# The tail of a two-layer kernel reordered: own part of the maxima ahead of the statistics, the sums behind the broadcast rows

## Chip, cores and metric

One core of one Trainium2 chip. The metric is the device time of one execution in microseconds (us). The engines are called TensorE (PE in the rows; PEld is its weight load), VectorE (DVE), ScalarE (ACT), GpSimd (POOL) and SyncE (SP, which issues most transfers).

## What is computed

x has 4 batches of 1024 rows and 512 columns, in fp32. Layer 0 is a two-layer network with a residual; 128 of its 512 output columns come from an expert that the batch's index chooses. Layer 1 scores every row, masks the scores by the batch's type, and pools the rows with the softmax of each row's masked scores.

```
h = gelu(x @ fc1_w.T + fc1_b)                       # 512 -> 2048, exact gelu
x = x + concat(h @ fc2_w.T + fc2_b, h @ experts_w[idx].T + experts_b[idx])
score = tanh(x @ W1 + b1) @ v                       # one number per row l
mask[j, l] = l <= j (type 0), l >= j (type 1), l != j (type 2)
p[j, :] = softmax over l of (score[l] where mask, else -1e30)
x[j] = x[j] + sum_l p[j, l] * x[l] / count(mask[j, :])
```

## The kernel before, in words

The batches run one after the other: a first one with its preparations ("first"), a loop over the other three, and a "tail" that has layer 1 of the last batch only. In the loop TensorE works on layer 0 of one batch, and layer 1 of the batch before is cut into small tasks between its products. In the tail no layer 0 is left to run beside these tasks. Every fp32 operand of a large product is split into a high part (a copy by ScalarE that rounds, helper `hi`, L988) and a low part (a subtraction by VectorE, helper `lo`, L1270), and a product is three matmuls (`three`, L770 to L774).

Layer 1 treats the 1024 rows as 8 chunks of 128 rows. The tasks, in the order of their data:

- `xn` (4 in the tail): chunks are transposed on TensorE (L865), and split into xnh and xnl; `full` keeps an unrounded copy for the last sum. xnl is the last reader of the bank.
- `attn`, `score`: tanh and the scores, s8. Behind `score` follows `maxima` (L1428): two scans of running maxima, F8 and G8, with the product DG between them.
- `stats`: three tiny products (L877 to L879), copied to st by VectorE (L1330). Then `row_maxima` (L1436): Ef and t88 from st, mc from t88, then m0 in three steps from s8, G8, F8 and the mask (L1441 to L1444), m8 from m0 and mc (L1446), and t88 less mc (L1447). The semaphore `chain` counts these 11 steps.
- `mT`: m8 gathered (L883, copied at L1335). `bc` 0 and 1: broadcast rows by eight transposes of mT (L889), from which VectorE makes the exponents of P (L1340, four per half) and of W (L1344).
- `expE`: ScalarE's exponential of Ef, then E's copies into the diagonals of E4 by VectorE: three casts (L1352) and a difference (the fourth copy).
- `sums`: 16 matmuls (L894, L895) of E4 with all chunks, copied to Bs.
- `expPW` h: exponentials of a half of P and W on ScalarE, their high parts, and the low parts Pl and Ws on VectorE.
- GpSimd's `row_sums` (L707) makes the terms of the denominators: FS and decay (L712, L713) when the scans are done, two operations behind m8 (L716, L717), and three at the end (L720 to L724) that need the scans of `scan` (L1373, L1375) and three exponentials of `expM`.
- `total` (L899), `den` (L1389), `rd` (L902, L1392, L1394): the reciprocals of the denominators.
- `pool` c: an own part of chunk c (`own_chunk`, three matmuls of P with x) and one matmul of Ws with Bs (L911) in one bank; then VectorE scales it and adds the row itself (L1406), and SyncE writes 256 KB out (L454).

The order in the tail is written out by hand. `TAIL_ORDER` (L98) is TensorE's order and deals the eight banks out; `TAIL_ACT` and `TAIL_DVE` are those of ScalarE and VectorE. Each engine works strictly in its order. `FILLS` matmuls without use (L955) stand ahead of `mT`. `FULL_BEFORE` says how many `full` copies TensorE awaits ahead of a task. The own parts of chunks 0 to 3 run ahead of `rd`, and those of 4 to 7 ahead of their own `pool`:

```
for c in range(BC) if task[0] == "rd" else [task[1]] if task[0] == "pool" and task[1] >= BC else []:
    own_chunk(kind, b, c, at(kind, "p", ("pool", c)))
```

The loop uses the same functions for its tasks, in the places of `POST_P` (L77): in step 3 the broadcast rows, `expE`, the exponentials, `scan` and the first `expPW`; behind them VectorE has the first `add` (L1465), which frees a bank for TensorE's product P2.

## Time and profile before

| | us |
|---|---|
| median of three runs | 778.43 (778.34 to 780.52) |
| the profiled execution | 778.85 |
| its span, first to last instruction | 777.1 |
| TensorE busy in the span | 762.0 (98%) |
| VectorE, ScalarE, GpSimd busy | 404.9, 386.7, 134.2 |
| mean granted clock of TensorE | 0.995 |

A stretch's row gives its length, then each engine's busy time with the number of its instructions, the granted clock of TensorE (1.00 is 2.4 GHz, 0.50 is 1.2 GHz), the share of the DMA engines and GB/s. A timeline's row gives start, duration, engine, line, operation and tiles; "x4" joins four alike, and what stands in brackets is the idle time before it and what ended it. Start times, not durations, give the pace, since neighbours overlap by about 0.1 us. In the chain a piece lasts until the next one takes over.

### The profile page before, as it was taken

To read this page: it belongs to the slowest core of one execution; us is meant where nothing else is said; L and a number is where in the kernel's file an instruction comes from. 1 tells how busy PE (TensorE), PEld (TensorE's weight loads), DVE (VectorE), ACT (ScalarE), POOL (GpSimd) and SP (SyncE) were. 2 spreads that over 40 slices of the span, in tenths; PEclk is the share of its full clock that TensorE was granted. 3 is DMA by queue.
4 is the path that set the end of the run, shared out by engine and by line. 5 is a ranking of instruction groups with operands and counts; after the bars stand their busy time and mean duration, and the time that the engine had idled before them with its cause. 6 is when DMAs were issued, how large, how long until landed. Compare 5 with 4: busy or idle time off the path is not lost.

```text
span 777.1 us, 11514 instructions
## 1 busy us (share of the span) xinstructions
PE 762.0 (98%) x3466; PEld 622.6 (80%) x3466; DVE 404.9 (52%) x713; ACT 386.7 (50%) x665; POOL 134.2 (17%) x199
## 2 busy tenths in 40 slices
PE   8999999999999999999999999999999999999977
PEld 5788888888888888888888888888888888888855
DVE  6965667573445333754536423377245532265676
ACT  6855665453546433543546633446354653344552
POOL 3273230400011121310001022040001111114011
PEclk9999999999999999999999999999999999999998
DMA  6899898877764568867776466885787466687712
GB/s 217 289 338 322 309 340 275 267 231 238 236 202 150 176 203 280 260 205 244 223 238 195 155 206 206 291 248 175 245 249 232 148 198 205 220 279 217 231 54 108
DMA packets 130714, 176.92 MB, mean 228 GB/s; under 512 B 10064, under 2 KB 97632, under 8 KB 130656
## 3 DMA queue, kind: packets, MB, share of 16 engines
q1 hardware_dynamic: 130496, 176.20, 71.2%
q8 instruction: 28, 0.46, 0.2%
q14 instruction: 30, 0.25, 0.1%
q0 software_dynamic: 160, 0.01, 0.0%
HBM read 136.33 MB, written 39.85 MB: 227 GB/s over the span
## 4 chain that ended last, share of the span: by engine, by line
PE 92%; DVE 3%; DMA 2%; ACT 1%; issue 1%; SPq 1%; DVEq 0%
PE y L772 15%; PE y L774 14%; PE y L773 14%; PE hA L772 7%; PE hA L774 7%; PE hA L773 7%; PE hF L772 6%; PE hF L774 5%; PE hF L773 5%; PE j L865 2%; DMA xrb<-in_x 1%; PE j L844 1%; PE j L842 1%; PE j L841 1%; DMA w2c<-exs 1%
## 5 line engine op out<-in xcount | busy, mean ns | idle before, releaser
L772 PE MATMUL y<-hs,w2c 128*128 128x512 f32 x512 | 201.9, 394 | 0.7 <-DMA w2c<-exs 0.5
L774 PE MATMUL y<-hs,w2c 128*128 128x512 f32 x512 | 199.6, 390 | 0.0
L773 PE MATMUL y<-hs,w2c 128*128 128x512 f32 x512 | 199.2, 389 | 0.0
L772 PEld LDWEIGHTS y<-hs,w2c 128*128 128x128 f32 x512 | 96.1, 188 | 22.8 <-DVE hs L1270 2.5
L774 PEld LDWEIGHTS y<-hs,w2c 128*128 128x128 f32 x512 | 96.1, 188 | 20.5
L773 PEld LDWEIGHTS y<-hs,w2c 128*128 128x128 f32 x512 | 96.2, 188 | 19.3
L772 PE MATMUL hA<-xch,w1c 128*128 128x512 f32 x252 | 99.5, 395 | 2.7 <-DVE w1c L1270 1.7
L774 PE MATMUL hA<-xch,w1c 128*128 128x512 f32 x252 | 98.2, 390 | 0.0
L773 PE MATMUL hA<-xcl,w1c 128*128 128x512 f32 x252 | 98.1, 389 | 0.0
L1042 ACT ACTIVATE hst<-hst,bcol 128x512 f32<-128x512 f32 x62 | 43.9, 721 | 85.4 <-DVE hst L1465 85.4
L1270 DVE TENSOR_TENSOR hs<-gb,hs 128x512 fp32r<-128x512 f32 x64 | 43.5, 716 | 64.6 <-ACT hs L988 64.6
L772 PE MATMUL hF<-xch,w1c 128*128 128x512 f32 x190 | 75.6, 398 | 0.3 <-issue 0.3
L774 PE MATMUL hF<-xch,w1c 128*128 128x512 f32 x190 | 74.1, 390 | 0.0
L773 PE MATMUL hF<-xcl,w1c 128*128 128x512 f32 x190 | 74.0, 389 | 0.0
L988 ACT ACTIVATE hs<-hst 128x512 fp32r<-128x512 f32 x64 | 40.4, 632 | 47.2 <-PE y L774 46.8
L1270 DVE TENSOR_TENSOR hs<-hst,hs 128x512 fp32r<-128x512 f32 x64 | 45.2, 706 | 35.9 <-ACT hs L988 34.9
L772 PEld LDWEIGHTS hA<-xch,w1c 128*128 128x128 f32 x252 | 47.3, 188 | 16.0 <-DVE w1c L1270 3.6
L774 PEld LDWEIGHTS hA<-xch,w1c 128*128 128x128 f32 x252 | 47.3, 188 | 10.0
L773 PEld LDWEIGHTS hA<-xcl,w1c 128*128 128x128 f32 x252 | 47.3, 188 | 9.3
L762 POOL TENSOR_TENSOR x1T<-x1T,xnl 128x512 f32<-128x512 f32 x24 | 30.8, 1290 | 136.7 <-DVE x1T L1409 136.7
L1465 DVE TENSOR_TENSOR hst<-hF,hst 128x512 f32<-128x512 f32 x31 | 21.4, 691 | 55.8 <-PE hF L774 55.3
L1042 ACT ACTIVATE gb<-gb,bcol 128x512 f32<-128x512 f32 x31 | 22.4, 724 | 54.3 <-DVE gb L1465 54.2
(286 smaller groups left out, 1093.9 us busy)
## 6 DMA issues: line engine op xcount, KB each, us to landing
w2c<-w2s SPq DMA_DIRECT2D x114, 384.0 KB, 3.5
w1c<-w1s SPq DMA_DIRECT2D x24, 768.0 KB, 4.4
w2c<-exs SPq DMA_DIRECT2D x114, 128.0 KB, 4.0
w1c<-w1s SPq DMA_DIRECT2D x48, 256.0 KB, 3.4
w1c<-w1s SPq DMA_DIRECT2D x24, 512.0 KB, 3.9
x1T<-in_x SPq DMA_DIRECT2D x32, 256.0 KB, 5.8
w1s<-w1c SPq DMA_DIRECT2D x8, 768.0 KB, 4.1
w2s<-w2c SPq DMA_DIRECT2D x16, 384.0 KB, 4.4
```

The source lines that it names most:

```text
L762: nc.gpsimd.tensor_tensor(oo[:, c % OUTS, :], oo[:, c % OUTS, :], xnl[:, c, :].bitcast(f32), ALU.add).then_inc(row_sum, 1)
L772: nc.tensor.matmul(ps, ah, bh, start=first, stop=False, skip_group_check=onto)
L773: nc.tensor.matmul(ps, ah, bl, start=False, stop=False, skip_group_check=onto)
L774: return nc.tensor.matmul(ps, al, bh, start=False, stop=last, skip_group_check=onto)
L841: nc.tensor.matmul(bank[:, :], W1h[:, dc, :], xh[:, dc, :], start=dc == 0, stop=False)
L842: nc.tensor.matmul(bank[:, :], W1l[:, dc, :], xh[:, dc, :], start=False, stop=False)
L844: last = nc.tensor.matmul(bank[:, :], W1h[:, dc, :], xl[:, dc, :], start=False, stop=dc == DC - 1)
L865: last = nc.tensor.transpose(bank[:, i * P:(i + 1) * P], x1T[:, i, c * P:(c + 1) * P], ident[:, :])
L988: return nc.scalar.activation(out_, in_, ACT.Copy)
L1042: nc.scalar.activation(tile, hA[:, :] if order == 4 else tile, ACT.Gelu, bias=bcol[:, R_FC1 + m:R_FC1 + m + 1]).then_inc(gelu_done, 1)
L1270: return nc.vector.tensor_tensor(out_, in_, hi_.bitcast(f32), ALU.subtract)
L1465: nc.vector.tensor_tensor(tile, bank[:, :], tile, ALU.add).then_inc(add_done, 1)
```

## The change

- `maxima` takes m0's three steps over from `row_maxima`, ahead of the statistics, with the wait for the mask. `row_maxima` makes m8 first, then Ef, then t88 less mc; m8 is step 9 of `chain` and Ef step 10.
- GpSimd starts `row_sums` at m8 rather than at the scans: its first two operations move behind it.
- E's three casts become one ScalarE copy of 128x24, behind Ef's exponential, waiting for it. VectorE keeps the fourth copy. E4 is one column per chunk wider so that the copy's pattern is regular.
- The exponentials of `expB` are three tasks now (`expS` the one of t88, first; `expF`, `expD`), and those of P and W, their high parts (`hiP`, `hiW`) and low parts (`loP`, `loW`) are tasks of their own. P's exponential waits for a new semaphore, `P_in`, that VectorE sets behind P's four operations, W's for the bank as before. `total` waits for the exponential of t88 only.
- TensorE: `sums` stands directly behind `bc` 1, and waits for the bank of each later chunk at that chunk's matmuls, not for the last one at its start. Own parts 0 to 3 run ahead of `total`; own part 4 and the four products of chunks 0 to 3 ahead of `den` and `rd`, own part 5 at `rd`, 6 and 7 at their chunks. All four `full` copies are awaited at `total`. The fills are 5, not 6.
- VectorE: `xn` 2 goes behind `mT`, `xn` 3 between the two `bc`, `scan` behind the first low parts. ScalarE: `expM` goes behind the copy of the sums.

The diff, cut to its core:

```diff
@@ -68,7 +68,7 @@
 UNITS = 2 * HC
-WARM, FILLS = 8, 6
+WARM, FILLS = 8, 5
 W2R = 4
 HSR = 3
...
@@ -97,16 +97,20 @@
 X_LOADS = {5: ((0, 1), 3, 2), 7: ((3,), 4, 3), 8: ((2,), 6, 3)}
 TAIL_ORDER = [("ysum", oc) for oc in range(OC)] + [("x1", oc) for oc in range(OC)] + [
     ("xn", 0), ("xn", 1), ("attn",), ("xn", 2), ("xn", 3), ("score",), ("stats",), ("expE",), ("mT",), ("bc", 0), ("bc", 1),
-    ("scan",), ("total",), ("expPW", 0), ("expPW", 1), ("sums",), ("den",), ("rd", 0, CH)] + [("pool", c) for c in range(CH)]
+    ("expPW", 0), ("sums",), ("scan",), ("expPW", 1), ("total",)] + [("pool", c) for c in range(BC)] + [
+    ("den",), ("rd", 0, CH)] + [("pool", c) for c in range(BC, CH)]
+OWN_BEFORE = {("total",): range(BC), ("pool", 0): [4], ("rd", 0, CH): [5], ("pool", 6): [6], ("pool", 7): [7]}
 TAIL_ACT = [("x1", oc) for oc in range(OC)] + [
-    ("xn", 0), ("xn", 1), ("attn",), ("xn", 2), ("xn", 3), ("full", 0), ("full", 1), ("expE",), ("expB",), ("full", 2), ("expM",),
-    ("full", 3), ("exp", 0), ("PW", 0), ("exp", 1), ("sums",), ("PW", 1)]
+    ("xn", 0), ("xn", 1), ("attn",), ("xn", 2), ("xn", 3), ("full", 0), ("full", 1), ("expE",), ("expS",), ("expF",), ("expD",),
+    ("full", 2), ("expP", 0), ("expW", 0), ("hiP", 0), ("hiW", 0), ("full", 3), ("expP", 1), ("hiP", 1), ("sums",), ("expM",),
+    ("expW", 1), ("hiW", 1)]
 TAIL_DVE = [("ysum", 0), ("ysum", 1), ("x1", 0), ("ysum", 2), ("x1", 1), ("ysum", 3), ("x1", 2), ("x1", 3), ("xn", 0),
-            ("xn", 1), ("score",), ("xn", 2), ("stats",), ("mT",), ("expE",), ("xn", 3), ("bc", 0), ("scan",), ("bc", 1),
-            ("expPW", 0), ("total",), ("sums",), ("expPW", 1), ("den",), ("rd", 0, CH)] + [("pool", c) for c in range(CH)]
-FULL_BEFORE = {("bc", 0): 1, ("bc", 1): 2, ("sums",): 3, ("rd", 0, CH): 4}
+            ("xn", 1), ("score",), ("stats",), ("mT",), ("xn", 2), ("expE",), ("bc", 0), ("xn", 3), ("bc", 1), ("loP", 0), ("loW", 0),
+            ("scan",), ("loP", 1), ("sums",), ("total",), ("loW", 1), ("den",), ("rd", 0, CH)] + [("pool", c) for c in range(CH)]
+FULL_BEFORE = {("bc", 0): 1, ("bc", 1): 2, ("total",): 4}
 def body(kind):
...
@@ -708,11 +715,10 @@
                 twice = lambda t: t[:, :].unsqueeze(1).to_broadcast([P, 2, P])
-                gate(pool, chain, b * NCHAIN + (BOTH - NCHAIN))
+                gate(pool, chain, b * NCHAIN + (MAX - NCHAIN))
                 nc.gpsimd.tensor_tensor(upto(FS), twice(s8), upto(FG), ALU.subtract).then_inc(den_in, 1)
                 nc.gpsimd.tensor_tensor(decay[:, :, :], short_of(FG), upto(FG), ALU.subtract).then_inc(den_in, 1)
                 gate(pool, den_in, b * NIN + (2 - NIN))
-                gate(pool, chain, b * NCHAIN + (MAX - NCHAIN))
                 nc.gpsimd.tensor_tensor(short_of(FG), short_of(FG), twice(m8), ALU.add).then_inc(den_in, 1)
                 nc.gpsimd.tensor_tensor(m0[:, :], s8[:, :], m8[:, :], ALU.add).then_inc(den_in, 1)
                 gate(pool, den_exp, b * NEXP + (6 - NEXP))
...
@@ -889,8 +895,9 @@
                         last = nc.tensor.transpose(bank[:, i * P:(i + 1) * P], mT[:, c:c + 1].to_broadcast([P, P]), ident[:, :])
                 elif task[0] == "sums":
                     pe.wait_ge(Elo, b)
-                    wait_used(pe, kind, b, at(kind, place, ("xn", CT - 1)))
                     for c in range(CH):
+                        if c >= CT:
+                            wait_used(pe, kind, b, at(kind, place, ("xn", c - CT)))
                         nc.tensor.matmul(bank[:, :], E4[:, c, :], xnh[:, c, :], start=(c == 0), stop=False)
                         last = nc.tensor.matmul(bank[:, :], E4[:, c, :], xnl[:, c, :], start=False, stop=(c == CH - 1))
                 elif task[0] == "total":
...
@@ -955,8 +962,7 @@
                                 nc.tensor.matmul(idle[:, :], W1h[:, 0, :], x1he[:, 0, :], start=True, stop=True)
                         if task in FULL_BEFORE:
                             pe.wait_ge(xfull_done, FULL_BEFORE[task])
-                        for c in range(BC) if task[0] == "rd" else [task[1]] if task[0] == "pool" and task[1] >= BC else []:
+                        for c in OWN_BEFORE.get(task, []):
                             own_chunk(kind, b, c, at(kind, "p", ("pool", c)))
                         job(kind, b, "p", task, pos)
                     return
...
@@ -1115,28 +1121,48 @@
                 elif task[0] == "expE":
                     act.wait_ge(chain, b * NCHAIN + (EF - NCHAIN))
                     nc.scalar.activation(Ef[:, :], Ef[:, :], ACT.Exp).then_inc(exp_done, 1)
+                    act.wait_ge(exp_done, b * 5 - 4)
+                    hi(groups[:, :, 0:32 * (GROUPS - 1):32], Ef[:, :].unsqueeze(2).to_broadcast([P, CH, GROUPS - 1])).then_inc(Ehi, 1)
                 elif task[0] == "expB":
-                    exps_B(b)
+                    exp_seen(b)
+                    exp_terms(b)
+                    exp_decay(b)
+                elif task[0] == "expS":
+                    exp_seen(b)
+                elif task[0] == "expF":
+                    exp_terms(b)
+                elif task[0] == "expD":
+                    exp_decay(b)
                 elif task[0] == "expM":
                     exps_M(b)
                 elif task[0] == "expPW":
-                    exp_PW(kind, b, place, task[1])
-                    split_PW(kind, b, task[1])
-                elif task[0] == "exp":
-                    exp_PW(kind, b, place, task[1])
-                elif task[0] == "PW":
-                    split_PW(kind, b, task[1])
+                    exp_P(b, task[1])
+                    exp_W(kind, b, place, task[1])
+                    split_PW(kind, b, task[1], 0)
+                    split_PW(kind, b, task[1], 1)
+                elif task[0] == "expP":
+                    exp_P(b, task[1])
+                elif task[0] == "expW":
+                    exp_W(kind, b, place, task[1])
+                elif task[0] in ("hiP", "hiW"):
+                    split_PW(kind, b, task[1], task[0] == "hiW")
                 elif task[0] == "sums":
                     hi(Bs[:, :], bank[:, :]).then_inc(sumhi, 1)
...
@@ -1328,7 +1358,6 @@
                         maxima(b)
                 elif task[0] == "stats":
                     nc.vector.tensor_copy(st[:, :], bank[:, 0:2 * CH + 1]).then_inc(used, 1)
-                    dve.wait_ge(mask_done, b)
                     wait_used(dve, kind, b, pos)
                     row_maxima(b)
                 elif task[0] == "mT":
...
@@ -1337,8 +1366,9 @@
                     for i in range(CT):
                         c = task[1] * CT + i
-                        nc.vector.scalar_tensor_tensor(Pf[:, c * P:(c + 1) * P], bank[:, i * P:(i + 1) * P], st[:, c:c + 1],
-                                                       TM[:, TRI], ALU.add, ALU.add)
+                        last = nc.vector.scalar_tensor_tensor(Pf[:, c * P:(c + 1) * P], bank[:, i * P:(i + 1) * P], st[:, c:c + 1],
+                                                              TM[:, TRI], ALU.add, ALU.add)
+                    last.then_inc(P_in, 1)
                     half = slice(task[1] * TT, (task[1] + 1) * TT)
                     cross = TM[:, P + task[1] * CT:P + (task[1] + 1) * CT]
                     nc.vector.scalar_tensor_tensor(
...
@@ -1346,30 +1376,21 @@
                         st[:, 2 * CH:2 * CH + 1], cross.unsqueeze(2).to_broadcast([P, CT, P]), ALU.add, ALU.add
                     ).then_inc(used, 1)
                 elif task[0] == "expE":
-                    diagonal = E4[:, :, :].rearrange("p c n -> p (c n)")
-                    dve.wait_ge(exp_done, b * 5 - 4)
-                    for gr in range(GROUPS - 1):
-                        last = nc.vector.tensor_copy(diagonal[:, 32 * gr:32 * gr + (CH - 1) * (P + 1) + 1:P + 1], Ef[:, :])
-                    last.then_inc(Ehi, 1)
                     dve.wait_ge(Ehi, b)
-                    gr = GROUPS - 1
-                    lo(diagonal[:, 32 * gr:32 * gr + (CH - 1) * (P + 1) + 1:P + 1], Ef[:, :],
-                       diagonal[:, 0:(CH - 1) * (P + 1) + 1:P + 1]).then_inc(Elo, 1)
+                    lo(groups[:, :, 32 * (GROUPS - 1)], Ef[:, :], groups[:, :, 0]).then_inc(Elo, 1)
                 elif task[0] == "expPW":
-                    h = task[1]
-                    half, cs = slice(h * TT, (h + 1) * TT), slice(h * BC, (h + 1) * BC)
-                    dve.wait_ge(PWhi, b * 4 + (2 * h - 3))
-                    lo(Pl[:, cs, :].rearrange("p c n -> p (c n)"), Pf[:, half], Ph[:, cs, :].rearrange("p c n -> p (c n)")
-                       ).then_inc(Plo, 1)
-                    dve.wait_ge(PWhi, b * 4 + (2 * h - 2))
-                    third = Ws[64:96, cs, :].rearrange("p c n -> p (c n)")
-                    lo(third, Wf[64:96, half], third).then_inc(Wlo, 1)
+                    split_P(b, task[1])
+                    split_W(b, task[1])
+                elif task[0] == "loP":
+                    split_P(b, task[1])
+                elif task[0] == "loW":
+                    split_W(b, task[1])
                 elif task[0] == "sums":
                     dve.wait_ge(sumhi, b)
                     lo(Bs[32:64, :], bank[32:64, :], Bs[32:64, :]).then_inc(used, 1)
                 elif task[0] == "scan":
-                    dve.wait_ge(den_exp, b * NEXP + (2 - NEXP))
+                    dve.wait_ge(den_exp, b * NEXP + (3 - NEXP))
                     nc.vector.tensor_tensor_scan(FS[:, 1:P + 1], decay[:, 0, :], FS[:, 1:P + 1], 0.0, ALU.mult, ALU.add
                                                  ).then_inc(den_scan, 1)
                     nc.vector.tensor_tensor_scan(FS[:, 2 * P + 1:P + 1:-1], decay[:, 1, ::-1], FS[:, 2 * P + 1:P + 1:-1], 0.0,
...
@@ -1409,6 +1430,18 @@
                     nc.vector.scalar_tensor_tensor(oo[:, c % OUTS, :], bank[:, :], rd[:, c:c + 1], xnh[:, c, :].bitcast(f32),
                                                    ALU.mult, ALU.add).then_inc(used, 1)
+            def split_P(b, h):
+                half, cs = slice(h * TT, (h + 1) * TT), slice(h * BC, (h + 1) * BC)
+                dve.wait_ge(PWhi, b * 4 + (2 * h - 3))
+                lo(Pl[:, cs, :].rearrange("p c n -> p (c n)"), Pf[:, half], Ph[:, cs, :].rearrange("p c n -> p (c n)")
+                   ).then_inc(Plo, 1)
+            def split_W(b, h):
+                half, cs = slice(h * TT, (h + 1) * TT), slice(h * BC, (h + 1) * BC)
+                dve.wait_ge(PWhi, b * 4 + (2 * h - 2))
+                third = Ws[64:96, cs, :].rearrange("p c n -> p (c n)")
+                lo(third, Wf[64:96, half], third).then_inc(Wlo, 1)
             def sum_of_x(b, k, x_):
                 to, a, c = {T1: (0, 1, 0), T3: (1, 3, 1), T2: (3, 3, 0), T4: (2, 2, 3)}[x_]
...
@@ -1433,17 +1466,19 @@
                 nc.vector.tensor_tensor_scan(G8[:, P - 1::-1], s8[:, P - 1::-1], s8[:, P - 1::-1], NEG, ALU.max, ALU.max
                                              ).then_inc(chain, 1)
+                dve.wait_ge(mask_done, b)
+                link(nc.vector.tensor_scalar(m0[:, :], s8[:, :], TM[:, NC:NC + 1], None, ALU.add), b, 4)
+                link(nc.vector.scalar_tensor_tensor(m0[:, :], G8[:, 1:P + 1], TM[:, NP_:NP_ + 1], m0[:, :],
+                                                    ALU.add, ALU.max), b, 5)
+                nc.vector.scalar_tensor_tensor(m0[:, :], F8[:, 0:P], TM[:, NS:NS + 1], m0[:, :], ALU.add, ALU.max
+                                               ).then_inc(chain, 1)
             def row_maxima(b):
+                link(nc.vector.tensor_tensor(t88[:, :], st[:, CH:2 * CH], TM[:, SEEN], ALU.add), b, 7)
+                link(nc.vector.reduce_max(mc[:, :], t88[:, :], AX.X), b, 8)
+                nc.vector.tensor_scalar(m8[:, :], m0[:, :], mc[:, :], -1.0, ALU.max, ALU.mult).then_inc(chain, 1)
                 nc.vector.tensor_tensor(Ef[:, :], st[:, 0:CH], st[:, CH:2 * CH], ALU.subtract).then_inc(chain, 1)
-                link(nc.vector.tensor_tensor(t88[:, :], st[:, CH:2 * CH], TM[:, SEEN], ALU.add), b, 5)
-                nc.vector.reduce_max(mc[:, :], t88[:, :], AX.X).then_inc(chain, 1)
-                link(nc.vector.tensor_scalar(m0[:, :], s8[:, :], TM[:, NC:NC + 1], None, ALU.add), b, 7)
-                link(nc.vector.scalar_tensor_tensor(m0[:, :], G8[:, 1:P + 1], TM[:, NP_:NP_ + 1], m0[:, :],
-                                                    ALU.add, ALU.max), b, 8)
-                link(nc.vector.scalar_tensor_tensor(m0[:, :], F8[:, 0:P], TM[:, NS:NS + 1], m0[:, :],
-                                                    ALU.add, ALU.max), b, 9)
-                nc.vector.tensor_scalar(m8[:, :], m0[:, :], mc[:, :], -1.0, ALU.max, ALU.mult).then_inc(chain, 1)
                 nc.vector.tensor_scalar(t88[:, :], t88[:, :], mc[:, :], None, ALU.subtract).then_inc(chain, 1)
             def split_w1(p, g):
```

## Rows read from the trace of the kernel before

**Rows 1.** Busy time by stretch: us, PE, PEld, DVE, ACT, POOL, granted clock, DMA share, GB/s.
```profile
371.00:556.00 185.00, 184.94 (x853) 152.26 (x851) 87.60 (x157) 87.96 (x149) 24.66 (x28) 1.00 0.71 222
...
740.00:758.00 18.00, 12.82 (x77) 10.13 (x75) 14.57 (x39) 11.61 (x24) 2.31 (x4) 0.96 0.12 40
758.00:777.10 19.10, 14.24 (x52) 11.09 (x52) 11.62 (x24) 4.28 (x8) 2.32 (x5) 0.86 0.29 110
```
**Rows 2.** The chain that ended last, in the tail: start us, us, what.
```profile
758.75 0.63 PE hF L894
...
768.87 4.70 DVE hst L1406 x7
```
**Rows 3.** Timeline of TensorE, 764 to 768.
```profile
764.50 0.39 PE L772 MATMUL y<-xnh,Ph 128*128 128x512 f32 x1
...
766.99 0.39 PE L774 MATMUL j<-xnh,Pl 128*128 128x512 f32 x1
767.98 0.36 PE L902 MATMUL y<-sel,m 128*128 128x8 f32 x2 [0.60 <-DVE m L1389]
```
**Rows 4.** Timeline, TensorE ahead of the sums, then the last of DVE.
```profile
754.25 1.06 PE L889 MATMUL j<-ident,mT 128*128 128x128 f32 x8 [0.35 <-DVE mT L1335]
...
758.18 0.57 PE L899 MATMUL hA<-DG,ones 128*128 128x8 f32 x2 [2.87 <-DVE DG L1378]
...
773.49 0.74 DVE L1406 SCALAR_TENSOR_TENSOR hst<-y,rd,hst 128x512 f32<-128x512 f32 x1
```
**Rows 5.** Timeline of DVE, 751 to 758: start us, us, instruction, [idle before].
```profile
751.06 0.18 DVE L1330 COPY st<-y 128x17 f32<-128x17 f32 x1
751.73 0.17 DVE L1438 TENSOR_TENSOR Ef<-st 128x8 f32<-128x8 f32 x1 [0.49 <-DVE st L1330]
...
752.09 0.28 DVE L1441 TENSOR_SCALAR m<-s,TM 128x128 f32<-128x128 f32 x1
...
753.17 0.29 DVE L1446 TENSOR_SCALAR m<-m,mc 128x128 f32<-128x128 f32 x1
...
753.94 0.17 DVE L1335 COPY mT<-y 128x8 f32<-128x8 f32 x1 [0.34 <-PE y L883]
754.02 0.74 DVE L1352 CAST E<-Ef 128x8 fp32r<-128x8 f32 x3
...
754.89 0.68 DVE L1270 TENSOR_TENSOR xnl<-y,xnh 128x512 fp32r<-128x512 f32 x1
755.49 1.12 DVE L1340 SCALAR_TENSOR_TENSOR x1T<-j,st,TM 128x128 f32<-128x128 f32 x4
...
757.18 0.41 DVE L1373 TENSOR_TENSOR_SCAN FS<-decay,FS 128x128 f32<-128x128 f32 x1
...
757.95 1.12 DVE L1340 SCALAR_TENSOR_TENSOR x1T<-j,st,TM 128x128 f32<-128x128 f32 x4
```
**Rows 6.** Timeline of GpSimd in the tail.
```profile
750.64 0.64 POOL L712 TENSOR_TENSOR FS<-s,FG 128x256 f32<-128x256 f32 x1 [41.06 <-DVE FG L1433]
751.24 0.61 POOL L713 TENSOR_TENSOR decay<-FG 128x256 f32<-128x256 f32 x1
...
759.64 1.00 POOL L724 TENSOR_TENSOR m<-m,FG 128x128 f32<-128x128 f32 x1 [0.18 <-POOL m L722]
```
**Rows 7.** Timeline of DVE at 760.
```profile
759.64 0.68 DVE L1270 TENSOR_TENSOR Pl<-x1T,Ph 128x512 fp32r<-128x512 f32 x1
760.35 0.83 DVE L1270 TENSOR_TENSOR Ws<-x1T,Ws 32x512 fp32r<-32x512 f32 x1
```
**Rows 8.** Busy time by stretch, as rows 1, where the clock fell and rose.
```profile
756.40:756.80 0.40, 0.00 (x0) 0.00 (x0) 0.40 (x2) 0.00 (x0) 0.00 (x0) 0.50 0.00 0
...
763.20:763.40 0.20, 0.20 (x3) 0.16 (x2) 0.00 (x0) 0.00 (x0) 0.00 (x0) 0.94 0.00 0
```
**Rows 9.** Timeline in the loop's first pass, TensorE, then DVE.
```profile
240.56 0.48 PE L772 MATMUL hF<-xch,w1c 128*128 128x512 f32 x1
...
238.93 0.69 DVE L1465 TENSOR_TENSOR hst<-hF,hst 128x512 f32<-128x512 f32 x1
```

42 lines of the change are left out of this document (25 added, 17 removed).

## Prediction

> **What bounds the kernel now.** I first read the table of stretches. In the loop TensorE is never short of work: 184.94 of the 185 us of one pass are busy, at the full clock [rows 1]. What comes after the loop is different. From 740 to the end at 777.10 TensorE is busy for 12.82 of 18.00 us and then 14.24 of 19.10 us, and its mean granted clock is 0.96 and then 0.86 [rows 1]. So the loop can only lose, and what the change can gain lies in these last 37 us. Next I read the chain that ended last. It goes through the small steps of the statistics on VectorE, through the 16 matmuls of the sums (758.75 until the first own-part matmul at 764.50), and then through the row work on VectorE from 768.87 [rows 2, 3]. That last piece runs at VectorE's own pace: from 768.87 to 773.49 are seven steps of 0.66 us, and the span ends 2.9 us after the last of them ends at 774.23 [rows 2, 4]. The change leaves these eight operations and their eight transfers alone, so whatever brings the start of the first of them forward (768.87) brings the end forward by as much. The question is when that operation can start.
>
> Ahead of it TensorE has one long hole: it waited 2.87 us for VectorE's DG and took up work at 758.18 [rows 4]. The sums were queued behind that one tiny product ("total"), though all that they need themselves was there long before.
>
> **The maxima, moved ahead of the statistics.** Now the statistics are copied at 751.06 and the last maximum, m8, ends at 753.17 + 0.29 = 753.46 [rows 5]. Between them stand three steps that need nothing of the statistics (752.09 to 753.17, 1.08 us), the subtraction for Ef (about 0.09), and an idle stretch of 0.49 us ahead of Ef [rows 5]. After the change the three steps run in the place that the low part of the third transposed chunk has now, from about 751.06 - 0.60 = 750.4 (0.60 is what its twin takes, 754.89 to 755.49 [rows 5]). They end at 751.5. The copy (0.2), the two steps with the statistics (751.73 to 752.09 less 0.09, so 0.27) and m8 (0.29) follow: m8 ends at 752.3. That is 1.15 us earlier. The idle 0.49 us falls beside two GpSimd operations (FS and decay, 750.64 to 751.85), which the change puts behind m8 [rows 6]. If the stall has another cause it stays, and this part is worth 0.65 us only.
>
> **VectorE's queue from there to the first low part of P.** The copy of mT now ends at 754.11, 0.65 us behind m8 [rows 5]; after the change at 752.95. Behind it come, in the new order: the low part of the third chunk 0.60; E's fourth copy 0.17 (the three casts go to ScalarE; casts and fourth copy hold 754.02 to 754.89 now, 0.87 us); the first half of the broadcast rows 755.49 to 757.18, 1.69; the low part of the last chunk 0.60; the second half 1.69; the low part of P 0.71 (759.64 to 760.35) [rows 5, 7]. The scan, 757.18 to 757.95, goes from the middle of this stretch to behind it [rows 5]. Sum: 752.95 + 0.60 + 0.17 + 1.69 + 0.60 + 1.69 + 0.71 = 758.4. I take 758.5. ScalarE has the first half exponentiated and copied well before: its inputs are there at 755.4 and it needs some 2.3 us for four operations of 512 columns. It gains one short copy of 24 columns, bounded by 0.1 us and by the 0.74 us that the three casts took on VectorE; I take 0.2, hidden, since it is busy for 11.61 of 18 us only [rows 1].
>
> **The sums.** They now wait only for E and for each chunk's own bank, and stand right behind the broadcast rows, whose transposes take 1.06 us from 0.14 us behind mT's copy (754.25 against 754.11) [rows 4, 5], so from 753.09 to 754.15. Full-clock pace is (766.99 - 764.50)/11 = 0.226 us a matmul [rows 3]; 16 of them are 3.6 us, so they end at 757.9. The last pair needs the last chunk's low part, which is there at 756.0. The order has two effects. The sums leave the path wholly, and the hole of 2.87 us is filled. Today the granted clock is down to 0.50 from 756.4, in that hole, and up again only at 763.2, inside the sums [rows 8]; these are the two levels 1.2 and 2.4 GHz. That cost 5.75 - 3.6 = 2.1 us. The one fill fewer takes 0.23 us of idle matmuls out of TensorE's queue; between the fills and the transposes it has only mT's small product, as now, and across that stretch the clock stays up today. I expect it to stay up throughout, since full matmuls follow at 754.15.
>
> **TensorE from the first low part of P.** Own parts of chunks 0 to 3 (12 matmuls), total, own part of 4 (3), the four products of chunks 0 to 3 (4), own part of 5 (3), then the denominators. 22 x 0.226 = 4.97, and total 0.36 like the same shape at 767.98 [rows 3]: 758.5 + 5.33 = 763.85. From the denominators' product to the first row operation pass 768.87 - 767.98 = 0.89 us [rows 2, 3]: it starts at 764.75. The own parts and products that remain for chunks 4 to 7 are ten matmuls, 2.3 us, and stay ahead of VectorE's 0.66 us a chunk. Gain: 768.87 - 764.75 = 4.1 us.
>
> **What runs beside it.** VectorE must have the denominators' input by 763.85. Low part of W 0.71 to 0.83, scan 0.77, low part of P 0.71, of the sums 0.71 take it to 761.4 [rows 5, 7]; total comes from TensorE at 758.5 + 2.7 + 0.4 = 761.6 and is taken in by about 762.3; the second low part of W (0.71) and the last step (0.36) end at 763.4. The margin is 0.4 us. GpSimd's chain is the other input. Its first four operations stand behind m8 together and take some 2.5 us at 0.61 to 0.64 us each, so till 755 [rows 6]. Its last three wait for exponentials of ScalarE that are put behind the sums' copy. By ScalarE's order (P's second half is there at 757.1; two operations of 0.57 us, the sums' copy 0.6, three short ones 0.9) they may start at about 760.4, an estimate, and three operations of 0.6 to 1.0 us take 2 to 3 us. That margin is between 0.9 us and nothing.
>
> One thing in this change collides. Beside VectorE's operations on two SBUF operands GpSimd's take longer: the operation at 759.64 took 1.00 us, longer than the 0.61 to 0.64 us of those with twice its elements; VectorE had an operation on two SBUF operands at 759.64 too, and the next of its kind took 0.83 us [rows 6, 7]. After the change E's fourth copy, at about 753.5, comes while decay is still being computed (to about 753.8), which by these rows costs nothing up to 0.3 us; I leave 0.1 in the rounding to 758.5. The Trainium skill, "SBUF — State Buffer", section "Who interferes with whom", calls the port pair that the two engines share an exclusive lock: the second of the two waits for the whole of the first. The 0.49 us ahead of Ef agree roughly: Ef started at 751.73 and decay is shown until 751.85. By that rule the sum would come out at the upper end, 0.2 us later.
>
> **The loop.** It uses the same code: three casts leave VectorE, ScalarE gains one copy and the low parts come no earlier. VectorE's first add ends at 239.62 and TensorE takes the freed bank at 240.56, so there is 0.94 us of cover [rows 9]; ScalarE's added copy eats at most 0.3 of it. I cost it at nothing.
>
> **The sum.** The profiled execution took 778.85 us with a span of 777.10; 778.85 - 4.1 = 774.75. It stands 0.42 above the median 778.43, which gives 774.3; rounded for the thin margins, 774.4.
>
> **Rivals.** (A) As above: chance 0.60, 773.9 to 775.1.
> (B) The denominators come late. GpSimd's last three operations or the second low part of W block each other, or the 0.49 us stall stays; 0.5 to 1.5 us are given back: 775.0 to 776.0, chance 0.20. For it: the margins of 0.4 and 0 to 0.9 us, and the 1.00 us operation.
> (C) The clock falls all the same at about 756.4 and stays down until 763.2. Then ten matmuls of the sums are done by 756.4 and six take 0.45 us each (to 759.1); nine of the twelve matmuls of own parts 0 to 3 are done by 763.2 and three follow at 0.226: 763.9 rather than 761.2. Of the gain 2.6 us go: 776.9 (776.1 to 777.6), chance 0.13. For it: TensorE's small work between 752.3 and 754.2. Against it: today's small work alone lowered it only at 756.4, over 1 us behind the last transpose, and now full matmuls follow at 754.15.
> (D) Slower. In the loop ScalarE's queue, with E's copy and the new waits of the exponentials for their inputs, holds the low part of W, and so the first add, past its 0.94 us of cover. The price is three times what goes beyond it; from a delay of 2.3 us on it outweighs the 4.1 us of the tail, and from 3.1 us on the kernel is slower by over 0.3%: chance 0.03, some 781. Nothing in the trace shows an addition of that size.
> (E) The sums' early start turns out to be hidden, since something else in front of the row work is late by as much: no change, 778, chance 0.04.
>
> **How the numbers follow.** About 0.3% (2.3 us) is what a measurement can tell from no change, so faster means below 776.1. A and B are wholly that: 0.80, with a small part of C 0.82; within 0.3%: the rest of C and E, 0.15; slower: D, 0.03. The range takes A, B and most of C: 773.7 to 776.9, which leaves out about 0.1 above it; its lower end lets go of the roundings (0.1 for E's copy, 0.1 in the last figure) and of 0.5 us more.
>
> **What would show it.** Right: no idle stretch of TensorE over 1.2 us between 750 and 764; the sums' matmuls at 0.226 us from about 754.2; a clock of 1.00 throughout; m8 done at 752.3; the low part of P at 757.8; the first row operation at about 764.8. Wrong: a granted clock of 0.50 inside the sums or own parts (C); VectorE's last step for the denominators waiting for GpSimd (B); idle TensorE in the loop (D).

## The result, and the profile after

The changed kernel takes 774.85 us (median of six runs, 773.78 to 776.04), the kernel before 778.38 us in the same comparison: a ratio of 0.9955, 95% interval 0.9944 to 0.9966, so 3.5 us less (2.6 to 4.4). The same code once more, in a later comparison, gave 774.95 us and 0.9950 (0.9934 to 0.9966). The forecast was 774.4 us, in the range 773.7 to 776.9. The profiled execution took 774.91 us with a span of 773.1.

The table of stretches of the changed kernel (columns as in rows 1):

```profile
371.00:556.00 185.00, 184.93 (x852) 152.01 (x852) 87.21 (x154) 87.78 (x149) 24.22 (x28) 1.00 0.73 221
...
740.00:758.00 18.00, 16.51 (x87) 13.39 (x87) 15.09 (x38) 12.65 (x24) 2.30 (x4) 0.91 0.10 36
758.00:777.00 19.00, 8.93 (x41) 6.88 (x39) 10.13 (x21) 3.59 (x9) 2.28 (x5) 0.86 0.30 112
752.00:753.00 1.00, 0.65 (x5) 0.59 (x6) 0.74 (x3) 0.79 (x4) 0.97 (x2) 0.95 0.00 0
756.00:757.00 1.00, 1.00 (x5) 0.78 (x4) 1.00 (x5) 1.00 (x3) 0.00 (x0) 0.85 0.00 0
```

The loop is as it was (184.93 of 185 us, against 184.94 [rows 1]). Between 740 and 758 TensorE is busy for 16.51 us in place of 12.82 [rows 1]: the hole of 2.87 us [rows 4] has gone, and the sums start in this stretch, where before they all came behind it. But the clock is not up throughout. It fell at about 752.9 and rose at about 756.3, while it was down from 756.4 to 763.2 before [rows 8].

The chain that ended last, tail (start us, us, what):

```profile
752.65 1.71 PE j L895 x8
...
758.77 0.23 PE hA L902
758.99 0.23 PE y L778
...
764.27 0.14 PE j L909 x2
...
764.93 2.73 DVE hst L1427 x4
```

Before, the chain went from VectorE's queue over the sums (758.75 [rows 2]) to the rows at 768.87 [rows 2]. Now TensorE holds it without a break from 752.65 to 764.27: transposes, sums, own parts, products, denominators. The first row operation starts at 764.93, 3.94 us earlier than 768.87.

The timeline of VectorE in the changed kernel, the steps that answer to rows 4, 5 and 7, with their idle time before them:

```profile
748.76 0.29 DVE L1356 TENSOR_TENSOR s<-y,s8a 128x128 f32<-128x128 f32 x1 [0.48 <-PE y L879]
...
750.70 0.35 DVE L1473 SCALAR_TENSOR_TENSOR m<-FG,TM,m 128x128 f32<-128x128 f32 x1
750.96 0.17 DVE L1360 COPY st<-y 128x17 f32<-128x17 f32 x1
...
751.57 0.28 DVE L1480 TENSOR_SCALAR m<-m,mc 128x128 f32<-128x128 f32 x1
...
752.34 0.17 DVE L1364 COPY mT<-y 128x8 f32<-128x8 f32 x1 [0.26 <-PE y L889]
...
753.02 0.25 DVE L1300 TENSOR_TENSOR E<-Ef,E 128x8 fp32r<-128x8 f32 x1
753.55 1.12 DVE L1369 SCALAR_TENSOR_TENSOR x1T<-j,st,TM 128x128 f32<-128x128 f32 x4 [0.28 <-PE j L895]
...
757.54 0.68 DVE L1300 TENSOR_TENSOR Pl<-x1T,Ph 128x512 fp32r<-128x512 f32 x1
...
761.88 0.17 DVE L1402 TENSOR_TENSOR t<-hF,t 128x8 f32<-128x8 f32 x1 [0.75 <-PE hF L906]
...
763.32 0.35 DVE L1410 SCALAR_TENSOR_TENSOR m<-s8a,Q,m 128x128 f32<-128x128 f32 x1 [0.36 <-POOL m L730]
764.43 0.17 DVE L1413 TENSOR_TENSOR rd<-j,TM 128x8 f32<-128x8 f32 x1 [0.77 <-PE j L909]
...
769.54 0.74 DVE L1427 SCALAR_TENSOR_TENSOR hst<-y,rd,hst 128x512 f32<-128x512 f32 x1
```

VectorE waits three times on the way to the rows: 0.75 us at 761.88, 0.36 at 763.32 and 0.77 at 764.43. The first two are new. The last is for the denominators' product, as before; there TensorE had itself waited 0.60 us before it could start that product at 767.98 [rows 3], and now it comes to it late with work of its own. Seven steps of the rows still take 769.54 - 764.93 = 4.61 us. To compare kernels I count from the start of the step that makes the scores s8 (748.76 here; 749.12 in the profile of before), since that moment lies between 748.2 and 751.0 us in the profiles of this study, whatever was changed behind it (748.76 and 749.67 for the same code). Where that comes from stays open. T is the time from there to the first row operation.

| profile | clock at 1.2 GHz | m8 starts | first low part of P | sums | first own part | denominators' product | T | rows |
|---|---|---|---|---|---|---|---|---|
| before | 7.3 to 14.1 | 4.05 | 10.52 | 9.48 to 15.4 | 15.38 | 18.86 | 19.75 | 4.62 |
| after | 4.1 to 7.5 | 2.81 | 8.78 | 5.25 to 10.1 | 10.07 | 15.35 | 16.17 | 4.61 |
| after, once more | 2.0 to 5.4 | 2.82 | 9.65 | 5.82 to 9.6 | 10.48 | 15.86 | 16.68 | 4.61 |
| e1, sums' order alone | none | 4.06 | 10.52 | 6.60 to 10.3 | 11.34 | 15.14 | 16.03 | 4.62 |
| e1 once more | 7.1 to 10.5 | 4.06 | 10.52 | 6.60 to 11.9 | 12.09 | 15.43 | 16.32 | 4.62 |
| e10, maxima and E alone | 8.0 to 11.5 | 2.82 | 9.19 | 7.94 to 13.3 | 13.27 | 16.75 | 17.64 | 4.61 |
| e2, maxima behind | 4.7 to 8.1 | 3.52 | 9.61 | 6.08 to 10.8 | 10.76 | 16.04 | 16.86 | 4.62 |
| e3, GpSimd early | 4.2 to 7.6 | 3.45 | 9.65 | 6.12 to 10.6 | 10.57 | 15.87 | 16.69 | 4.62 |
| e4, casts on VectorE | none | 2.82 | 9.29 | 5.53 to 9.3 | 10.11 | 15.52 | 16.33 | 4.62 |
| e5, denominators first | 14.8 to 18.2 | 2.82 | 8.55 | 4.71 to 8.4 | 9.38 | 14.46 | 15.40 | 5.73 |
| e6, two fills more | 2.5 to 5.9 | 2.81 | 9.82 | 6.10 to 9.8 | 10.65 | 16.02 | 16.83 | 4.62 |
| e7, waits taken out | 3.5 to 6.9 | 2.81 | 9.01 | 5.49 to 9.9 | 9.88 | 14.80 | 15.69 | 4.62 |
| e8, e7 with fills | none | 2.82 | 8.58 | 4.74 to 8.5 | 9.40 | 14.26 | 15.15 | 4.62 |
| e9, e7 with the scan earlier | 2.1 to 5.5 | 2.82 | 9.66 | 5.83 to 9.6 | 10.49 | 15.51 | 16.40 | 4.62 |

All in us behind the scores, from one profile each; "rows" is from the start of the first row operation to the start of the last. "clock at 1.2 GHz" is the low phase between the scores and the last row operation; a fall behind the last product is left out. The changed kernel once more has T 16.68 us, where I had expected 15.5 to 16.3: with the clock falling as early as 2.0 us, the fills and transposes ahead of the first low part are slowed too.

### The profile page after: what moved, and what is told of

Read it like the earlier page. It is cut to its first block, busy times and chain, and to the rows that moved or that the text cites. A ratio compares the mean times of both kernels' runs of the same rounds, so it can differ in the third digit from the quotient of the medians.

```text
span 773.1 us, 11505 instructions
## 1 busy us (share of the span) xinstructions
PE 760.9 (98%) x3465; PEld 621.8 (80%) x3465; DVE 403.2 (52%) x701; ACT 387.4 (50%) x669; POOL 131.8 (17%) x199
## 4 chain that ended last, share of the span: by engine, by line
PE 93%; DVE 3%; ACT 1%; DMA 1%; issue 1%; SPq 0%; DVEq 0%
PE y L778 15%; PE y L780 15%; PE y L779 15%; PE hA L778 7%; PE hA L779 7%; PE hA L780 7%; PE hF L778 5%; PE hF L780 5%; PE hF L779 5%; PE j L871 2%; PE j L848 1%; PE j L850 1%; PE j L847 1%; PE j L778 1%; PE j L779 1%; PE j L780 1%
## 5 line engine op out<-in xcount | busy, mean ns | idle before, releaser
L719 POOL TENSOR_TENSOR FS<-s,FG 128x256 f32<-128x256 f32 x4 | 2.6, 642 | 274.9 <-DVE Ef L1481 274.9
```

## What each part is worth

My theory was the prediction's: each part shortens one chain, and the shares add up. The rival that came up from the three waits above: the order of the sums on TensorE carries the gain, and what VectorE gains besides turns into waiting.

**e1: the sums' order alone.** Nothing of the change but this, in the kernel before (the second pair of lines moves a wait for a copy along with it):

```diff
-    ("scan",), ("total",), ("expPW", 0), ("expPW", 1), ("sums",), ("den",), ("rd", 0, CH)] + ...
+    ("sums",), ("scan",), ("total",), ("expPW", 0), ("expPW", 1), ("den",), ("rd", 0, CH)] + ...
-FULL_BEFORE = {("bc", 0): 1, ("bc", 1): 2, ("sums",): 3, ("rd", 0, CH): 4}
+FULL_BEFORE = {("bc", 0): 1, ("bc", 1): 2, ("total",): 3, ("rd", 0, CH): 4}
```

> The kernel before with one part alone: in the tail TensorE runs the sums directly behind the broadcast rows, ahead of total. Nothing else is changed. I measure T, from the start of the step that makes the scores s8 on VectorE to the start of the first row operation (19.75 us before, 16.17 us after), since it leaves out what the head of the kernel does. Theory A, the order of TensorE carries nearly all: the sums run from about 6.5 us behind the scores, the denominators wait only for the second low part of W, T is 15.8 to 16.8 us, and the kernel takes about 775. Theory B, by the sum of the prediction, in which the 1.15 us of the maxima and the 0.7 us of the casts count in full: T is 16.17 + 1.85 = 18.0 us, about 776.7.

It took 775.48 us, ratio 0.9955 (0.9941 to 0.9969), T 16.03 us. I ran it again beside the changed kernel:

> The kernel of e1 once more (before with the sums' order alone), on the same chip as the changed kernel: if the order of the sums carries all of the gain, the two differ by less than 0.1%, and T is again 16.0 us with no idle of TensorE ahead of the sums over 1.1 us.

It gave 0.9949 (0.9937 to 0.9962) and T 16.32 us, beside 0.9950 and 16.68 us of the changed kernel in the same comparison. Theory B's 18.0 us is out. TensorE and VectorE of the first e1 profile:

```profile
756.28 0.47 PE L894 MATMUL hA<-xnh,E 128*128 128x512 f32 x1 [0.41 <-DVE xnl L1270]
...
761.02 0.47 PE L772 MATMUL y<-xnh,Ph 128*128 128x512 f32 x1 [0.75 <-DVE Pl L1270]
...
764.82 0.36 PE L902 MATMUL y<-sel,m 128*128 128x8 f32 x2 [0.81 <-DVE m L1389]
...
754.50 0.17 DVE L1335 COPY mT<-y 128x8 f32<-128x8 f32 x1 [0.34 <-PE y L883]
...
760.20 0.68 DVE L1270 TENSOR_TENSOR Pl<-x1T,Ph 128x512 fp32r<-128x512 f32 x1
...
764.32 0.35 DVE L1389 SCALAR_TENSOR_TENSOR m<-s8a,Q,m 128x128 f32<-128x128 f32 x1
...
765.71 1.41 DVE L1406 SCALAR_TENSOR_TENSOR hst<-y,rd,hst 128x512 f32<-128x512 f32 x2
```

The sums run before the first low part of P is made (760.20), no clock is lost, and from 754.50 to the denominators' last step at 764.32 its timeline shows no idle stretch of VectorE: its queue is the path. TensorE has only 12 matmuls between that low part and the denominators and waits for VectorE there (0.81 us at 764.82).

**e10: the rest alone.** The changed kernel's code with the tail's orders of before, except that the third chunk's low part stays behind mT; so the maxima, GpSimd's later start and E's copies are what is left of the change, with its one fill fewer and the new waits of some tasks (P's exponential for `P_in`, `total` for one exponential only).

> The counterpart of e1: the changed kernel's code with the tail's orders of before (sums behind total, own parts and denominators as before, expM and scan in their old places), so that only the maxima ahead of the statistics (with the third chunk's low part behind mT) and E's copies by ScalarE are left of the change. If the gains of the parts were additive in the changed kernel, T would be 16.17 + (19.75 - 16.03) = 19.9 us here, no gain at all, since e1 alone gave 16.03. Theory: these parts are worth 1.24 (m8) and 0.6 (casts) us as long as VectorE's queue leads to total and the sums behind it: T about 17.9 us, clock effects of up to 1 us either way, and about 776.5 us. Rival: they are worth nothing anywhere, T 19.5 to 19.9.

It took 777.84 us, 0.9986 (0.9975 to 0.9997), T 17.64 us. The theory's 17.9 us is met in T, its 776.5 us is missed. By the ratio the time moved by 1.1 us (0.2 to 1.9), less than the 2.1 us of T; its one profile has the clock down for 3.4 us only, where before's has 6.8. The granted clock of the runs says how far that is usual: it never exceeds 0.996 in the 61 runs of the kernel before that stand beside the experiments, and it is 0.997 in four of e10's ten runs. Those four took 776.45 to 777.46 us, the other six 777.3 to 780.93. TensorE still has the hole ahead of total:

```profile
754.87 1.06 PE L894 MATMUL j<-ident,mT 128*128 128x128 f32 x8 [0.35 <-DVE mT L1363]
758.70 0.36 PE L905 MATMUL hA<-DG,ones 128*128 128x8 f32 x2 [2.77 <-DVE DG L1398]
758.91 0.68 PE L900 MATMUL hF<-xnh,E 128*128 128x512 f32 x1
```

So one part alone takes 3.7 us off T (e1), the other 2.1 us (e10), and the changed kernel, with both, 3.6 and 3.1 us in its two profiles. They are not additive.

**e2: the maxima behind the statistics, in the changed kernel** (in short).

```diff
 def maxima(b):
-    dve.wait_ge(mask_done, b)
-    (m0's three steps)
 def row_maxima(b):
+    dve.wait_ge(mask_done, b)
     (t88, mc)
+    (m0's three steps)
     (m8, Ef, t88 less mc)
```

> The changed kernel with m0's three steps behind the statistics again (GpSimd still starts at m8, the rest of the change stays). By the prediction m8 comes 1.08 us later and T grows by as much, to 17.2 us. Rival: the low part of P was ready 0.6 us before TensorE took it up in the changed kernel's profile, so only 0.5 us show, T 16.6 us; if TensorE's clock stays up in one profile and not in the other this can move by 0.6 us either way.

776.74 us, 0.9976 (0.9966 to 0.9986), T 16.86 us, between the theory's 17.2 and the rival's 16.6. m8 starts 0.71 us later, not 1.08: the copy of the statistics then waits for TensorE rather than for m0's steps. T is 0.69 us longer than in the first profile of the changed kernel and 0.18 longer than in the second. The ratio says that the place of the maxima is worth something in the changed kernel (0.9976 against 0.9955 and 0.9950, from different comparisons whose intervals meet at 0.9966). That doesn't go against e1: beside the changed kernel's longer queue ahead of the denominators the maxima pay for what that queue costs, and e1 has neither.

**e4: E's copies as casts on VectorE, in the changed kernel** (in short).

```diff
-act: hi(groups[:, :, 0:32 * (GROUPS - 1):32], Ef[:, :].unsqueeze(2).to_broadcast(...))
+dve: for gr in range(GROUPS - 1):
+         last = nc.vector.tensor_copy(groups[:, :, 32 * gr], Ef[:, :])
```

> The changed kernel with E's three copies as casts on VectorE again. By the prediction VectorE's queue ahead of the broadcast rows is longer by 0.5 to 0.8 us and T is 16.7 to 17.0 us. Rival: hidden by the 0.6 us in which the low part of P lay ready, T within 0.2 us of 16.17. The casts read and write SBUF beside GpSimd's first operations, so one of them may take 0.4 us rather than 0.17.

776.18 us, 0.9966 (0.9954 to 0.9979), T 16.33 us. That looks like the rival, but the clock stayed up in this profile and fell in that of after. With the clock up the first low part of P starts 8.55 (e5) and 8.58 us (e8) behind the scores with the copy on ScalarE, and 9.29 us with the casts: 0.7 us, as forecast. Only part of it is the casts:

```profile
753.67 0.40 DVE L1379 CAST E<-Ef 128x8 fp32r<-128x8 f32 x3
754.11 0.68 DVE L1298 TENSOR_TENSOR E<-Ef,E 128x8 fp32r<-128x8 f32 x1
```

They hold VectorE for 0.44 us; the other 0.3 us are the fourth copy behind them, which took 0.68 us, where it takes 0.25 us in the changed kernel (753.02 above). It ran beside GpSimd's third operation, which started at 754.08.

**e3: GpSimd's first two operations at the scans.** The wait for m8 goes back behind them:

```diff
-gate(pool, chain, b * NCHAIN + (MAX - NCHAIN))
+gate(pool, chain, b * NCHAIN + (BOTH - NCHAIN))
 FS, decay
+gate(pool, chain, b * NCHAIN + (MAX - NCHAIN))
```

> The changed kernel with GpSimd's first two operations (FS, decay) at the end of the two scans again, as before the change; the maxima stay ahead of the statistics. In the profile of before VectorE stood idle for 0.49 us ahead of Ef while the second of these ran, and in that of after no such idle time is there. If the two engines hinder each other, m0's three steps (they read SBUF) now fall beside these two operations and m8 starts 0.4 to 1.2 us later than 2.81 us behind the scores. If the 0.49 us had another cause, m8 starts at 2.8 us as in the changed kernel.

Its time is that of a single run, 775.86 us. m8 started 3.45 us behind the scores, 0.64 later. VectorE, then GpSimd:

```profile
750.74 0.75 DVE L1472 SCALAR_TENSOR_TENSOR m<-FG,TM,m 128x128 f32<-128x128 f32 x1
751.53 0.58 DVE L1474 SCALAR_TENSOR_TENSOR m<-FG,TM,m 128x128 f32<-128x128 f32 x1
...
750.71 0.64 POOL L719 TENSOR_TENSOR FS<-s,FG 128x256 f32<-128x256 f32 x1 [41.51 <-DVE m L1471]
751.30 0.66 POOL L720 TENSOR_TENSOR decay<-FG 128x256 f32<-128x256 f32 x1
```

m0's last two steps took 0.75 and 0.58 us beside GpSimd's two, where the last took 0.35 us in the changed kernel (750.70 above). e2 shows the other side. There the statistics' copy is followed at once by the next step, with GpSimd's two behind m8:

```profile
751.15 0.18 DVE L1360 COPY st<-y 128x17 f32<-128x17 f32 x1 [0.60 <-PE y L885]
751.37 0.17 DVE L1473 TENSOR_TENSOR t<-st,TM 128x8 f32<-128x8 f32 x1
```

The idle 0.49 us stand in both profiles of e1, where GpSimd's decay runs beside them as before, and in no profile in which it runs behind m8. So the prediction's reading of the 0.49 us ahead of Ef [rows 5, 6] holds.

## Where the gain of the other parts went

**e5: the denominators ahead of the products.**

```diff
-... ("total",)] + [("pool", c) for c in range(BC)] + [("den",), ("rd", 0, CH)] + [("pool", c) for c in range(BC, CH)]
+... ("total",)] + [("den",), ("rd", 0, CH)] + [("pool", c) for c in range(CH)]
-OWN_BEFORE = {("total",): range(BC), ("pool", 0): [4], ("rd", 0, CH): [5], ("pool", 6): [6], ("pool", 7): [7]}
+OWN_BEFORE = {("total",): range(BC), ("pool", 4): [4], ("pool", 5): [5], ("pool", 6): [6], ("pool", 7): [7]}
```

> The changed kernel with the last part undone: the denominators' product stands ahead of the products of chunks 0 to 3, and own parts 4 to 7 ahead of their own chunks, as before the change. By the prediction the own parts and products ahead of the denominators are TensorE's work on the path, and without them VectorE's last step, not TensorE, decides: that step ended 0.43 us ahead of the denominators' product, so T is 15.7 to 15.8 us, better than the changed kernel. Rival: the products of chunks 0 to 3 ahead of the denominators are needed, since else VectorE waits for them chunk by chunk: T 16.2 us or the same start with idle time between the row operations.

776.21 us, 0.9973 (0.9963 to 0.9984): worse by its median, though T is shorter (15.40 us). That is the rival's second branch. TensorE and the stretch behind it, then VectorE:

```profile
763.30 0.36 PE L909 MATMUL y<-sel,m 128*128 128x8 f32 x2 [1.96 <-DVE m L1410]
...
765.28 0.63 PE L778 MATMUL j<-xnh,Ph 128*128 128x512 f32 x1
...
764.00:766.00 2.00, 2.00 (x6) 1.60 (x5) 1.85 (x4) 0.00 (x0) 0.00 (x0) 0.50 0.10 30
...
767.21 0.75 DVE L1427 SCALAR_TENSOR_TENSOR hst<-j,rd,hst 128x512 f32<-128x512 f32 x1 [0.24 <-PE j L918]
```

TensorE waited 1.96 us for the denominators, the clock went to 0.50, and its four matmuls a chunk (0.43 us each) did not keep up with VectorE: the row operations took 5.73 us. The order alone isn't it: the kernel before has the same order there, and with the clock up its rows took 4.62 us. T and rows together are 21.13 us, against 20.78 and 21.29 in the two profiles of the changed kernel, whose clock had fallen earlier. The shorter T is mostly not this edit's: 0.69 us of the 0.77 lie ahead of the first own part (9.38 against 10.07), where the clock stayed up in this profile and not in the other. From the first own part to the first row it is 6.02 us here and 6.10 there. With the clock up until the first own part, as here, the changed kernel would come to 9.38 + 6.10 + 4.61 = 20.1 us, an estimate, and that is 1.0 us less than e5. So the products that the change puts ahead of the denominators cost 0.1 us, and keep TensorE busy through the wait: that part of the change pays by the clock. The runs bear it out: a low phase of 3.4 us takes 3.4 x 0.5 / 773 = 0.002 off the mean granted clock of a run, and none of e5's ten runs has 0.999, against five of the changed kernel's twelve.

**e6: two fills more**, between mT's product and the transposes.

> The changed kernel with two fills more, placed between mT's product and the transposes, where TensorE waits for VectorE's copy of mT. In the profile of the changed kernel the clock fell at about 752.95, four transposes into the broadcast rows, and rose at about 756.4; the sums ended 0.6 us after the first low part of P was there. Theory: with the clock up T is 15.6 us (16.17 less 0.57), the fills themselves costing up to 0.2 us, and the granted clock of the runs is 0.999 in more of them than 3 of 6. Rival: the clock falls all the same now and then, as it falls in before's 6.8 us only with the 2.87 us hole, and the medians do not differ.

775.87 us, 0.9968 (0.9959 to 0.9978), T 16.83 us: no gain, and neither branch as I had it: the granted clock is 0.999 in one run of nine. In the profile the clock fell among the fills (2.5 us behind the scores); the five then took 1.90 us, the two added ones 1.20, and the transposes had to wait for them. The changed kernel's second profile shows the same, and more plainly:

> The changed kernel once more, beside e9 and e1 on the same chip: ratio to the kernel before 0.995 to 0.9965, T 15.5 to 16.3 us according to where the clock falls.

```profile
750.74 0.39 PE L883 MATMUL y<-DG,ones 128*128 128x8 f32 x2 [1.14 <-DVE DG L1465]
...
751.43 2.26 PE L962 MATMUL j<-x1e,W1h 128*128 128x512 f32 x5
753.49 0.43 PE L889 MATMUL y<-sel,m 128*128 128x8 f32 x2
...
749.00:750.00 1.00, 0.60 (x11) 0.17 (x9) 0.49 (x3) 1.00 (x4) 0.00 (x0) 1.00 0.00 0
750.00:751.00 1.00, 0.26 (x3) 0.26 (x3) 0.96 (x4) 1.00 (x3) 0.00 (x0) 1.00 0.00 0
752.00:753.00 1.00, 1.00 (x3) 0.77 (x3) 0.89 (x6) 0.47 (x2) 0.05 (x1) 0.50 0.00 0
```

The five fills took 2.26 us in place of 1.42, since the clock fell in them, and mT's product, whose m8 was done at 752.77, ran at 753.49. Before, m8 came behind the fills; now that it starts 1.24 us sooner, fills at 1.2 GHz eat 0.7 us of that.

**e7: the three waits of VectorE taken out** (in short; own part 5 stands ahead of chunk 4's product, not at chunk 5 as the expectation has it).

```diff
 TAIL_ACT: ("full", 2), +("expM",), ("expP", 0), ... ("sums",), -("expM",), ("expW", 1), ("hiW", 1)
 TAIL_DVE: ("loP", 1), ("sums",), +("loW", 1), ("total",), -("loW", 1), ("den",)
 TAIL_ORDER: ("total",), ("den",), ("rd", 0, CH), then all ("pool", c)
 OWN_BEFORE = {("total",): range(BC), ("rd", 0, CH): [4], ("pool", 4): [5], ("pool", 6): [6], ("pool", 7): [7]}
```

> The changed kernel with four moves: ScalarE's four exponentials for the denominators (expM) directly behind its third full copy rather than behind the copy of the sums; VectorE's second low part of W ahead of total; the denominators' product ahead of all products, with own part 4 ahead of it; own part 5 at chunk 5. In the changed kernel VectorE stood idle for 0.75 us (for total), 0.36 us (for GpSimd's last operation) and 0.77 us (for the denominators' product) on the way to the first row operation, 1.9 us in all. Theory: these waits are what keeps the changed kernel from being faster than the sums' order alone; with them gone T is 14.6 to 15.0 us, the row operations take 4.62 us as ever, and the time is about 773.6. Rival: as in the run with the denominators first, TensorE waits for them and its clock falls, and the row operations take 5.7 us in place of 4.6: T + rows stays at 20.5 to 21.

**e8** adds e6's two fills:

> The kernel of e7 with the two fills of e6 as well. If the clock matters there only as 0.6 us on the way to the first own part, and that own part is on the path, T is shorter than that of e7 by 0 to 0.6 us where e7's clock fell, and the same where it did not. Theory: 773.3 us, granted clock 0.999 in nearly all runs.

e7 took 775.25 us, 0.9960 (0.9947 to 0.9972), T 15.69 us; e8 775.66 us, 0.9966 (0.9955 to 0.9978), T 15.15 us. I had expected 773.6 and 773.3 us, and the clock up in nearly all runs of e8; it has 0.999 in three of seven. In both T is shorter than in the changed kernel and the rows take 4.62 us; in neither is the median time. Most of e8's shorter T is the clock's again: from the first own part to the first row e7 and e8 take 5.81 and 5.75 us, the changed kernel 6.10, so the four moves are worth 0.3 us, where I had reckoned on up to 1.5. In e7 VectorE, then GpSimd:

```profile
765.14 0.35 DVE L1410 SCALAR_TENSOR_TENSOR m<-s8a,Q,m 128x128 f32<-128x128 f32 x1 [0.59 <-POOL m L730]
...
762.19 1.14 POOL L726 TENSOR_TENSOR FG<-FG,FS 128x256 f32<-128x256 f32 x1 [5.59 <-DVE DG L1399]
763.51 0.97 POOL L728 TENSOR_TENSOR m<-m,FG 128x128 f32<-128x128 f32 x1 [0.18 <-POOL FG L726]
```

A wait for GpSimd stays (0.59 us): its first two operations behind the scan took 1.14 and 0.97 us, beside VectorE's low parts.

**e9: the scan between the first low parts**, so that GpSimd starts earlier (`("loP", 0), ("scan",), ("loW", 0), ("loP", 1)` on VectorE).

> The kernel of e7 (exponentials early, second low part of W ahead of total, denominators ahead of the products) with VectorE's scan between the first low parts of P and of W. In e7's profile VectorE still waited 0.59 us for GpSimd's last operation: its three operations started 0.25 us behind the scan, took 1.14, 0.97 and 0.45 us, the first two beside operations of VectorE on two SBUF operands. The scan 0.71 us earlier brings that chain forward by as much. Theory: VectorE does not wait for GpSimd any more, T is 15.0 to 15.2 us where the clock fell as in e7 (15.69) and 14.7 where it stayed up, the row operations take 4.62 us. Rival: the two engines block each other in other places instead and T stays at 15.5 to 15.7.

775.58 us, 0.9960 (0.9942 to 0.9977), T 16.40 us, longer than both branches had it. Its profile has the clock down from 2.1 us behind the scores, with fills of 2.20 us and mT's copy 0.91 us late:

```profile
754.25 0.17 DVE L1364 COPY mT<-y 128x8 f32<-128x8 f32 x1 [0.91 <-PE y L889]
...
761.88 1.12 DVE L1300 TENSOR_TENSOR Pl<-x1T,Ph 128x512 fp32r<-128x512 f32 x1
...
765.03 0.35 DVE L1410 SCALAR_TENSOR_TENSOR m<-s8a,Q,m 128x128 f32<-128x128 f32 x1
...
761.19 1.26 POOL L726 TENSOR_TENSOR FG<-FG,FS 128x256 f32<-128x256 f32 x1 [5.41 <-DVE DG L1399]
```

VectorE's last step no longer waits for GpSimd, but its low part at 761.88 took 1.12 us beside GpSimd's 1.26 us: the rival's other place. None of e7, e8 and e9 can be told from the changed kernel by its ratio, and none beats it. Whether they would with a steady clock is open, but the record gives a hint. In runs with a granted clock of 0.999 or more no low phase of 3.4 us can hide. The median of such runs is 775.5 us for e1 (four runs of the two comparisons), 774.8 for the changed kernel (five) and 774.3 for e7, e8 and e9 together (seven). The runs within each group spread over 1.5 to 2.3 us, so this is a hint and no more.

## Point by point

- The sum, 4.1 us: the first row operation came 3.94 us earlier in the profile, of which 3.58 us are T and 0.36 the earlier scores; the medians say 3.5 (2.6 to 4.4) and, once more, 3.9. Right in size, and in part by luck: in T, which leaves the head out, the gain is 3.58 us in one profile and 3.07 in the other, where the sum says 4.1, and the first profile's scores happened to come 0.36 us earlier.
- The maxima: m8 was to come 1.15 us earlier and starts 1.24 us earlier. That the 0.49 us were GpSimd's doing was right (e3).
- VectorE's queue: the first low part of P was forecast at 757.8, 8.68 us behind the scores; it started at 8.78, and at 8.55 and 8.58 where the clock stayed up. E's fourth copy took 0.25 us rather than 0.17 beside decay, within the bounds that were left for it.
- The clock: forecast 1.00 throughout. This step failed. It fell 4.1 us behind the scores in one profile of the changed kernel and 2.0 in the other, both ahead of rival C's place. The argument that across that stretch "the clock stays up today" took one profile's moment for a property of the stretch. The low phase lasted 3.4 us, not C's 6.8, and cost about 0.5 us rather than C's 2.6. The sums ended at 10.1 us where 8.8 was forecast, the first own part started at 10.07 where 9.4 was (the low part lay ready for 0.6 us), T was 16.17 where 15.6 was. So C's sign, a clock of 0.50 inside the sums, was there, and the time still fell into A's range.
- TensorE behind the first own part: forecast 5.33 us to the denominators' product, measured 5.28.
- What runs beside: the margins were thin as said. VectorE waited for total (its start had slipped with the own parts), for GpSimd (0.36 us, rival B's mechanism and sign) and for TensorE; the denominators' last step ended 0.4 us ahead of their product, and so cost nothing.
- The loop: costed at nothing, and TensorE's idle time there is the same. Rival D is out.
- What the prediction did not see: the change's other parts buy nothing on top of the sums' order as they are put together here. Its sum follows one chain through the new order, and that was sound; but it counted m8 and the casts as gains of the change, and it did not work out where the chain ends with the sums' order alone. There the denominators wait for 12 matmuls behind the first low part; in the changed kernel total, an own part, four products and another own part stand ahead of them too (22 matmuls), and the scan stands behind the first low part. What VectorE gains ahead of that low part (10.52 less 8.78, 1.7 us) is given back between it and the denominators' product (4.6 us in e1, 6.6 us after). That is rival E's case, for these parts and not for the sums. Two things make up the 1.9 us: the order, 1.5 (with the clock up the low part starts at 8.55 and the denominators' product would stand at 9.38 + 5.28 = 14.66, so 6.1 us), and the clock, 0.5. By the same working the changed kernel would reach its rows at 9.38 + 6.10 = 15.5 us with the clock up, against 16.03 in e1: the other parts are worth 0.5 us there, an estimate from three profiles that no profile of the changed kernel shows, and where the clock falls early, as in both profiles of the changed kernel, they lose it again.
